# GNN layer on one Trainium2 core: the two identity products that add the cross sums become one of 192 columns

## The reference

```
s1 = concatenate([xs[:, :8], xd[:, :8]])             # 16 scalars
v1 = the 24 others of each row, as 16 vectors
v_t = a1 * (einsum('eu,euw->ew', s1, Wsv)[:, :, None] * sh1[:, None, :]
            + einsum('euk,euw->ewk', v1, Wvs))
...
edge_out = concatenate([tanh(scal), vecs * tanh(gates)]) * weight
x = layernorm(x + segment_sum(edge_out, dst))
```

## Time and profile before

| | us |
|---|---|
| runs | 6491.57, 6505.99, 6510.45 |
| median | 6505.99 |
| the profiled execution | 6485.43 |
| its span, first to last instruction | 6483.5 |

### The profile page before, as it was taken

The page is one execution under the profiler, slowest core; times in us unless marked ns, Lnnn a source line. Parts: engine busy times, 40 slices in busy tenths (PEclk is TensorE's granted clock), DMA queues, the critical chain, the costliest instruction groups (busy, mean ns, idle before and its releaser), DMA issues.

```text
span 6483.5 us, 222832 instructions
## 1 busy us (share of the span) xinstructions
PE 5938.8 (92%) x69422; PEld 5751.0 (89%) x69422; DVE 5877.3 (91%) x7326; ACT 3998.5 (62%) x12507; POOL 4979.5 (77%) x6875
## 2 busy tenths in 40 slices
PE   4999999999999999999999999999999999999997
PEld 3989989989899989998999999899998988999897
DVE  7989989989999999998999999999999999999998
ACT  5666666656666666666666666666666666666664
POOL 6777778777777777787777777787787777777774
PEclk9999999999999999999999999999999999999998
DMA  5434434434444444443444444444444444444442
GB/s 140 90 85 86 90 86 89 88 82 88 87 85 91 87 86 86 89 90 84 90 85 86 88 88 86 87 91 87 90 88 85 88 87 86 87 90 87 89 87 55
DMA packets 1671120, 569.95 MB, mean 88 GB/s; under 512 B 1535146, under 2 KB 1619083, under 8 KB 1670536
## 3 DMA queue, kind: packets, MB, share of 16 engines
q1 hardware_dynamic: 1567911, 516.43, 36.1%
q0 software_dynamic: 103168, 53.03, 5.1%
HBM read 302.19 MB, written 7.26 MB: 48 GB/s over the span
## 4 chain that ended last, share of the span: by engine, by line
PE 59%; issue 16%; DVE 11%; another core or an unknown queue 5%; ACT 4%; POOL 3%; DVEq 1%; SPq 1%; DMA 0%; ACTq 0%; POOLq 0%
PE p L1043 31%; PE pw L1038 16%; DVE prods L1300 3%; PE p L1131 3%; PE ph L1026 2%; POOL nodes L654 2%; DVE sv L1331 2%; PE ph L1015 1%; PE p L1126 1%; ACT off_hot L870 1%; DVE prods L1338 1%; DVE prods L1348 1%; PE p L1074 1%; PE p L1077 1%
## 5 line engine op out<-in xcount | busy, mean ns | idle before, releaser
L1043 PE MATMUL p<-identity,prods 128*128 128x128 f32 x29016 | 3599.8, 277 | 232.2 <-ACT gates_t L835 191.9
L654 POOL DMA_INDIRECT nodes<-x_rows,idx x3224 | 3104.5, 963 | 708.9 <-issue 590.1
L1043 PEld LDWEIGHTS p<-identity,prods 128*128 128x128 f32 x29016 | 3244.4, 144 | 262.4 <-issue 214.7
L1038 PE MATMUL pw<-w_stack,hid_t 128*128 128x128 bf16 x22568 | 1684.2, 221 | 176.5 <-issue 82.2
L1038 PEld LDWEIGHTS pw<-w_stack,hid_t 128*128 128x128 bf16 x22568 | 1438.2, 100 | 257.0 <-issue 111.9
L1293 DVE TENSOR_TENSOR prods<-pw,V 128x2048 f32<-128x2048 f32 x403 | 923.0, 2290 | 273.7 <-remote 175.0
L1338 DVE TENSOR_TENSOR prods<-pw,M 128x1024 f32<-128x1024 f32 x806 | 976.9, 1212 | 5.4 <-PE pw L1038 3.3
L870 ACT ACTIVATE off_hot<-node_iota,off_base 128x42 f32<-128x42 f32 x3216 | 747.0, 317 | 0.0
L1348 DVE TENSOR_TENSOR prods<-pw,VT 128x1536 f32<-128x1536 f32 x403 | 705.2, 1750 | 20.6 <-remote 18.0
L1315 DVE TENSOR_TENSOR prods<-pw,S 128x1024 f32<-128x1024 f32 x403 | 490.7, 1218 | 123.8 <-PE pw L1038 117.8
L1307 DVE TENSOR_TENSOR prods<-pw,S 128x1024 f32<-128x1024 f32 x403 | 490.8, 1218 | 14.0 <-remote 13.9
(11 more groups left out here) (138 smaller groups left out, 8483.5 us busy)
## 6 DMA issues: line engine op xcount, KB each, us to landing
dstb<-in_dst SPq DMA_DIRECT2D x403, 504.0 KB
nodes<-x_rows,idx POOLq DMA_INDIRECT x3224
emb_stack<-emb_parts SPq DMA_DIRECT2D x2418, 20.0 KB
emb<-in_emb_t SPq DMA_DIRECT2D x403, 40.0 KB
hid_t<-hid_parts SPq DMA_TRANSPOSE x806
idx<-in_src SPq DMA_DIRECT2D x403, 4.0 KB
xw<-x SPq DMA_DIRECT2D x403, 7.9 KB
vecs<-in_vec SPq DMA_DIRECT2D x403, 12.0 KB
```

Of the source, the lines that this page charges most:

```text
L654: nc.gpsimd.indirect_dma_start(nodes[:, p, t, side, :], None, x_rows, bass.IndirectOffsetOnAxis(ap=idx[:, p, side, t:t + 1], axis=0)).then ...
L1038: mm = nc.tensor.matmul(pw[:, slot, t, :], hid_t[:, layer, a.par, t, :], w2_stack[:, lo:lo + W], start=True, stop=True)
L1043: return nc.tensor.matmul(out, column, identity[:, :], start=first, stop=last, is_transpose=True)
```

## The change

In `vector_sums_turned` the two plain products with the identity, 128 and 64 columns of svr, become one of 192 columns. It comes first and opens the accumulation over all 192 columns of vs_ps; the transposing product of the first half of vs_t and the halves product add to it. All waits stay ahead of the first product, and vs_back is given by the last.

```diff
                 pe.wait_ge(svr_done, a.n(1, 1))
-                added(vs_ps[:, 0:P], vs_t[:, 0, :], True, False)
-                nc.tensor.matmul(vs_ps[:, 0:P], identity[:, :], svr[:, 0:2, :, :].rearrange("p k t w -> p (k t w)"),
-                                 start=False, stop=True)
-                nc.tensor.matmul(vs_ps[:, P:P + P // 2], vs_t[:, 1, :], halves[:, :], start=True, stop=False)
-                nc.tensor.matmul(vs_ps[:, P:P + P // 2], identity[:, :], svr[:, 2, :, :].rearrange("p t w -> p (t w)"),
-                                 start=False, stop=True).then_inc(vs_back, 1)
+                nc.tensor.matmul(vs_ps, identity[:, :], svr[:, :, :, :].rearrange("p k t w -> p (k t w)"),
+                                 start=True, stop=False)
+                added(vs_ps[:, 0:P], vs_t[:, 0, :], False, False)
+                nc.tensor.matmul(vs_ps[:, P:P + P // 2], vs_t[:, 1, :], halves[:, :], start=False, stop=True
+                                 ).then_inc(vs_back, 1)
```

## The result

| | before | after |
|---|---|---|
| median of 20 runs, us | 6497.23 | 6473.42 |
| lowest to highest, us | 6463.21 to 6530.23 | 6436.11 to 6505.68 |
| the profiled execution, us | 6485.43 | 6436.11 |
| its span, us | 6483.5 | 6434.2 |
| its mean granted TensorE clock | 0.977 | 0.983 |

The ratio is 0.996 with a 95% interval of 0.9941 to 0.998: 24 us faster, between 13 and 38 us. Two things are to be kept in mind. The profiled execution of the changed kernel is the fastest of its 20, and the two profiled executions lie 49 us apart, twice the difference of the medians. And all of this holds for the chips of those runs; on a chip of the experiments the same two kernels take 6061 and 6059 us and don't differ.

The account below looks back on a forecast made before the run. A relay between TensorE and VectorE was taken as the bound, with TensorE's block one leg. Removed 0.22 less added 0.11 us, times 403 periods and 0.7, made 31 us off the 6505.99 us median: 6475 us, range 6436 to 6516.

Parts of the forecast that it names:

- Removed 0.22 us: TensorE block: dropping the 64-column identity product L1077 saves 0.22 us a period, 89 us of TensorE time over 403 periods.
- Added 0.11 us: TensorE block: widening the identity product from 128 to 192 columns raises its pair from 0.22 to 0.33 us a period.
- The loads don't set the pace: Rival on TensorE: stationary-tile loads set the pace, 192 columns still take 0.22 us; 6444 us; 0.10 together with fewer stalls.
- second change of kind: Block order: plain, transposing, plain has two changes instead of one, giving back 0 to 0.06 us a period; taken as nothing.
- The prediction's own sign that its mechanism is wrong: Profile after: a 192-column pair costing over 0.44 us would make the merged product dearer than the two old ones.
- the forecast's own formula: Whole kernel: 403 periods times the block's saving (0.11 us forecast) times path share 0.7, making 31 us.
- 0.7 of the block's length goes into the time: Critical chain: TensorE's block is on the path in about 295 of 403 periods, taken as share 0.7.
- More long stalls: Rival at waits for gates_t: shifted timing redeals stalls, 3.4 us each; 20 more give 6543 us, 10 fewer 6441; slower 0.12.
- Held signals: Rival: SyncE's six-transfer burst L415 holds TensorE's signals back, so only 3 us is gained, 6503 us; chance 0.30.
- The SyncE queue could be the pace: Within the held-signals rival: SyncE is almost continuously at work, so it and not TensorE could set the pace.
- Next in line: VectorE becomes late next; 0.11 us fits most periods' room, and L1293's idle time falls or stays if the forecast is right.
- the held case: Sign of held signals: TensorE's waits for VectorE's second product L1300 grow by up to 44 us while the time stays.

Follow-up runs that it names:

- merged_last: Kernel before with only the merging: vs_t, halves product, then one 192-column identity product last; on a prompt-signal chip nothing differed (6058 to 6061 us).
- base: The kernel before, unedited, run once more on another chip with late signals: 6485.66 us.
- two_scatter: Kernel before with two of the eight scatter products per super-block, on a prompt-signal chip: 25 us slower than the kernel before at 6059.45 us.
- before_extra: Kernel before with one more 64-column identity product at the head of the block, on a prompt-signal chip: ratio 0.9997.
- two_first: Kernel before with only the order changed, both identity products first, four products as before; on a prompt-signal chip nothing differed (6058 to 6061 us).

## Why the prediction came out as it did

The forecast was 6475 us and the median of 20 is 6473.4; the sum was 31 us and the measured difference is 24 (from 6497.23, the median of 20; from the 6505.99 of the three runs shown, the median that the forecast started at, the same 6473 us would be 33). The number is right. Its steps are right in part, and the agreement is partly luck.

**Removed 0.22 us: right.** L1077's two records took 112 ns each to the next start, 0.224 us.

**Added 0.11 us: right in its rate, wrong in its place.** The stream pitch of a 192-column record is 162 ns (163 in merged_last), where 0.85 ns a column had given 165. The loads don't set the pace. Nor does the estimate from the Trainium skill hold (TensorE: Matmul & The Clock Gate, Back-to-back issue gap), 89 ns for 192 columns: for these float32 records it is 162. But the first record of the pair has 267 ns, 105 more, since it now stands right behind the scatter. vs_t, which stood there, gives back 56 (165 down to 109). So the pair grows by 205 ns, and the sum is 224 - 205 + 56 = 75 ns a period instead of 110. This is the prediction's "second change of kind", 0 to 0.06 us; it took nothing and the rows show 0.05. The prediction's own sign that its mechanism is wrong was a pair of over 0.44 us, and its place to look was the chain, which has 0.52. Start to start, by which two old products took 0.224 us each, 0.448 together, the pair takes 0.43, so the merged product is hardly cheaper than the two; what is gained comes to the most part from vs_t, which no longer follows the scatter. merged_last, with the wide product last, doesn't escape it: there the first record behind the halves has 218 ns, and the fill behind the second comes 163 after it, 845 in all. With the measured block the forecast's own formula gives 403 x 0.075 x 0.7 = 21 us.

**The step that doesn't hold: 0.7 of the block's length goes into the time.** It was worked out from a share printed as 1%, which may be anything from 0.5 to 1.5%, and from four periods; the whole chain of that trace holds L1077 in 247 of 403 periods, 0.61, which makes 18 us of the 21. That is a size. The passing on itself is contradicted by how the profiled pair came by its 49 us: the ordinary periods are 0.21 us longer, not shorter, the signal of the fill comes no earlier in the median (3.04 us for 2.98), and what is gained comes from the long ones. On the two chips with prompt signals 66 or 74 ns less and 221 ns more a period are all worth nothing. On a chip with late signals both pairs of traces have the gain in the long periods and none in the ordinary ones. No run there varied the block's length without its order, so why the long ones are fewer stays open.

**More long stalls: the right mechanism, the other sign.** The prediction counted waits for gates_t and took them as cards dealt anew. They fell from 87 to 28. Its price was 3.4 us for one stall; there are 33 fewer periods over 16.5 us and 118 us less of excess (278 us over a length of 15.2 us before, 161 after), 3.6 us for each, part of which is that the ones that stay are shorter. The ordinary periods gave more than half of it back: before, 317 of them were 0.19 us under 15.2 us, after, 350 are 0.02 over it, some 67 us. 118 less 67 is about the pair's 49 us. The prediction gave this side a part of 0.10 and its forecast 0.48, so that the time fell where the forecast had it is luck in this: 21 us by its own formula, and 24 measured by what looks like another way. The clock goes along with it: of the 20 runs of the changed kernel the three fastest (6436 to 6452 us) have a mean granted clock of 0.982 to 0.983, the three slowest (6495 to 6506) 0.976 to 0.977. The profiled run of before, at 0.977, took 6485 us, no more than those three. By that one run the kernel before isn't slower than the changed one at an equal clock, and what the change brings would be fewer stalls. On the chip of base the kernel before took 6457, 6465 and 6480 us at 0.978 and 6457 at 0.980, where the changed kernel has 6455 to 6490 at 0.978 to 0.980. But these are other chips and few runs, so it is a hint and not shown.

**Held signals: falls as a cause, stands as an observation.** TensorE's signals are late in the first trace, but not because of the six transfers: they are as late with one. In one thing this rival was right: in the median period what the block gives up doesn't reach VectorE. "The SyncE queue could be the pace" fits the prompt chips: 31 to 39% of the chain is SyncE's queue there, and no change of the block moves the time. The Trainium skill, Perfetto Trace Analysis, section Tensor Engine Instruction, tells that the recorded end of a matmul is an estimate and that the semaphore follows the acknowledged write to PSUM. Both traces can be read by it (14 ns and 1.75 us behind the same record), but no row says what delays the acknowledgement on one chip and not on another. Whether the products really end later there, or only their signals come later, no trace here shows.

**Next in line.** VectorE's idle time ahead of its first product fell, as forecast, by 96.5 us, and TensorE's wait for its second one rose by 24 us of the 44 that the held case had allowed. A part of the gain turned up as 39 us more ahead of L1347.

## What to carry to other kernels

When a matmul is widened and moved, price it by its stream pitch and by its new neighbour: here 64 columns more cost 0.05 us a record, and the first plain product behind a stream of narrow ones another 0.1. Before a leg of a relay is priced by its share of the chain, look whether that chain is the same on another chip: the kernel before had TensorE with 59% of it at 6.49 ms, and the changed one, whose block alone differs, SyncE's queue with 39% at 6.07 ms. Taking work from an engine that then idles can lower its clock and lose time, as two_scatter did; count the time at the lower level beside the waits. And before a count of long periods is taken as a result, move the line that makes them long: here 85 and 52 at 16.5 us were 90 and 82 at 16.

## What the runs showed of the hardware

- The kernel before takes 6486 us (one chip) and 6497 us (the result) in the median, and 6059 and 6061 on two other chips. The difference goes with how late TensorE's signals come behind the recorded ends: 14 ns for each on the fast ones; on the slow ones 1.5 to 1.6 us for the fill of kind 0, 1.7 to 1.9 us for vs_back, yet 14 ns for two of the seven fills and for vs_sum (medians). It isn't the SyncE queue's burst of six. Small dense products of the scatter come just ahead of these two; whether they are the cause wasn't settled. The signals of the fill of kind 1 and of L1093, which come behind the gate sums, are later still in the first trace, 2.5 and 2.3 us (medians).
- Two transposing float32 products start 109 ns apart at 128 columns, two records of one plain product 112 ns at 128 and 162 ns at 192. Behind the scatter the first plain record takes 48, 101 or 105 ns more than in the stream, at 64 (before_extra), 128 (two_first) and 192 columns.
- TensorE's granted clock fell to its lower level behind an idle time of 1.28 us, and a kernel with less work for TensorE was 0.4% slower, with such a stretch in 46 of its 47 long periods. The idle time alone doesn't bring it: that trace has 148 of over 1 us, and 48 stretches at the lower level.
